# Rows of negated maxima of a second attention: identity products at partitions 32 to 96 exchanged for transposes at partition 0

## The reference, cut to what matters

```python
q = (src @ Wq).reshape(Bb, Tt, H, DH).transpose(0, 2, 1, 3)
k = (src @ Wk_c @ Wk).reshape(Bb, Tt, H, DH).transpose(0, 2, 1, 3)
v = (src @ Wv_c @ Wv).reshape(Bb, Tt, H, DH).transpose(0, 2, 1, 3)
q = _apply_rope(q, sin, cos)
k = _apply_rope(k, sin, cos)
attn = jnp.einsum('bhqd,bhkd->bhqk', q, k) / np.sqrt(DH).astype(np.float32)
attn = jax.nn.softmax(attn, axis=-1)
sa = jnp.einsum('bhqk,bhkd->bhqd', attn, v)
```

## Time and profile before

| | before |
|---|---|
| median of 3 runs | 423.7 us (422.77 to 424.12) |
| the profiled execution, its own time | 420.97 us |
| its span, first to last instruction | 419.2 us |
| mean granted TensorE clock | 0.917 |
| busy: PE / PEld / DVE / ACT / POOL | 363.3 / 195.0 / 297.1 / 234.7 / 162.3 us |
| second attention in the span | about 205 to 353 us |

### The profile page before, as it was taken

The page is one execution under the profiler, slowest core; times in us unless marked ns, Lnnn a source line. Parts: engine busy times, 40 slices in busy tenths (PEclk is TensorE's granted clock), DMA queues, the critical chain, the costliest instruction groups (busy, mean ns, idle before and its releaser), DMA issues.

```text
span 419.2 us, 12911 instructions
## 1 busy us (share of the span) xinstructions
PE 363.3 (87%) x5331; PEld 195.0 (47%) x5331; DVE 297.1 (71%) x538; ACT 234.7 (56%) x489; POOL 162.3 (39%) x342
## 2 busy tenths in 40 slices
PE   8666779999999999997989889779989998999993
PEld 4232345767676767654655333312333333463441
DVE  5995865766878788888698987656787752426565
ACT  2623675767676667666744676545767884422200
POOL 7272163737677576554570111200001160143423
PEclk9985556999999999999999999955999999989997
DMA  7400000000000001000000000500000000000000
GB/s 236 126 22 4 1 5 4 5 23 6 4 9 3 8 6 30 4 4 2 3 5 2 4 25 0 163 1 2 2 0 3 3 0 2 0 2 0 0 25 27
DMA packets 11992, 8.09 MB, mean 19 GB/s; under 512 B 4446, under 2 KB 11022, under 8 KB 11806
## 3 DMA queue, kind: packets, MB, share of 16 engines
q1 hardware_dynamic: 11934, 7.27, 6.0%
HBM read 5.94 MB, written 0.52 MB: 15 GB/s over the span
## 4 chain that ended last, share of the span: by engine, by line
PE 56%; DVE 21%; issue 7%; ACT 7%; POOL 3%; SPq 2%; DMA 2%; ACTq 0%; POOLq 0%; DVEq 0%
PE ps L1236 8%; PE ps L1331 7%; PE ps L1149 5%; PE ps L1198 5%; PE ps L1180 4%; PE ps L1161 4%; DVE m_qk L863 3%; PE ps L1207 3%; PE ps L1223 3%; PE ps L1119 3%; ACT arena L696 3%; PE ps L1021 3%; PE ps L1216 2%; DVE m_qk L860 2%; DVE k_op L820 2%
## 5 line engine op out<-in xcount | busy, mean ns | idle before, releaser
L860 DVE TENSOR_REDUCE m_qk<-ps 128x2 f32<-128x1024 f32 x64 | 76.9, 1220 | 18.9 <-PE ps L1119 18.7
L863 DVE TENSOR_REDUCE m_qk<-ps 128x2 f32<-128x1024 f32 x64 | 76.8, 1219 | 17.6 <-PE ps L1207 17.3
L696 ACT ACTIVATE arena<-ps 128x512 f32<-128x512 f32 x128 | 69.5, 595 | 23.3 <-PE ps L1161 22.7
L711 ACT ACTIVATE arena<-ps 128x512 f32<-128x512 f32 x128 | 67.7, 600 | 17.6 <-PE ps L1223 16.9
L606 POOL TENSOR_TENSOR arena<-arena,eb 128x256 f32<-128x256 f32 x64 | 46.9, 733 | 59.5 <-ACT eb L684 33.2
L684 ACT ACTIVATE eb<-ps 128x512 f32<-128x512 f32 (+1 forms) x64 | 31.3, 542 | 28.7 <-PE ps L1149 28.7
L449 POOL TENSOR_SCALAR var<-mv 128x1 f32<-128x1 f32 (+1 forms) x14 | 2.7, 194 | 107.0 <-ACT eb L753 71.7
L1236 PE MATMUL ps<-arena,v_sb 128*20 128x256 f32 x512 | 41.1, 407 | 2.4 <-DVE arena L868 2.4
L1180 PE MATMUL ps<-arena,v_sb 128*20 128x128 f32 x1024 | 40.8, 284 | 0.0
L607 POOL TENSOR_TENSOR arena<-arena,eb 128x192 f32<-128x192 f32 x64 | 38.6, 603 | 0.0
L1149 PE MATMUL ps<-q_op,rel_k 49*128 49x24 bf16 (+1 forms) x1024 | 31.0, 222 | 6.4 <-ACT arena L696 3.2
(11 more groups left out here) (217 smaller groups left out, 537.9 us busy)
## 6 DMA issues: line engine op xcount, KB each, us to landing
rel_v<-in_relv_ext SPq DMA_DIRECT2D x1, 1024.0 KB, 7.9
eb<-in_w SPq DMA_DIRECT2D x2, 512.0 KB, 5.9
x_sb<-in_x SPq DMA_DIRECT2D x2, 256.0 KB, 3.1
q_op<-farT SPq DMA_DIRECT2D x32, 3.0 KB
q_op<-farT SPq DMA_DIRECT2D x32, 1.5 KB
out<-x_sb SPq DMA_DIRECT2D x8, 64.0 KB, 1.6
rows<-in_rows SPq DMA_DIRECT2D x1, 448.0 KB, 5.7
sel<-in_sel SPq DMA_DIRECT2D x1, 384.0 KB, 3.8
```

What stands on the lines that cost most here:

```text
L696: act.activation(p_ring[:, k % SLOTS_P, e, :], ps[:, bank, :], ACT.Exp).then_inc(sm["bank_free"], 1)
L711: act.activation(p_ring[:, v % RING, e, :], ps[:, bank, :], ACT.Exp).then_inc(sm["bank_free"], 1)
L860: dve.tensor_reduce(m_qk[:, u, n:H:PAIRS], ps[:, banks, :], AX_X, ALU.max).then_inc(sm["pair_free"], 1)
L863: dve.tensor_reduce(m_qk[:, IT * b + n, 2 * p:2 * p + 2], ps[:, banks, :], AX_X, ALU.max).then_inc(sm["pair_free"], 1)
```

## The change

The step `neg` uses the transpose form of the matmul in place of the product with the identity, and always writes partitions 0 and 1 of the bank. ACT reads them there and writes one of three blocks of 512 columns at partitions 0 and 1 in SBUF, where before it wrote partitions 32, 64 or 96 of one block. To have room for the three blocks, `m_rel`, `ends` and `far_bf` of the first attention become views of one tile `far_sb`, and the blocks lie over them; `neg_mT` keeps a tile of its own. The list of steps, the banks, the semaphores and what waits for them stay as they are: each engine issues as many instructions as before, in the same order (PE 4 for each of the 16 steps `neg`).

```diff
-        m_rel = sb("m_rel", [P, NT, H])
         m_rel_bf = sb("m_rel_bf", [P, NT, H], BF16)
-        ends = sb("ends", [P, NT, 2, H])
-        far_bf = sb("far_bf", [P, NT, 2, 2, 3, PAIRS], BF16)
+        far_sb = sb("far_sb", [P, 768])
...
-        neg_rows = sb("neg_rows", [P, 2, 2, P], BF16)
+        neg_mT = sb("neg_mT", [H, 2, 2, P], BF16)
...
-        neg_mT, nm_T = neg_rows[0:H], neg_rows[:, :, :, :].rearrange("p k n t -> p (k n t)")
+        ends = far_sb[:, 0:256].rearrange("p (u c h) -> p u c h", u=NT, c=2)
+        m_rel = far_sb[:, 256:384].rearrange("p (u h) -> p u h", u=NT)
+        far_bf = far_sb[:, 384:768].bitcast(BF16).rearrange("p (u c e s a) -> p u c e s a", u=NT, c=2, e=2, s=3)
+        nm_T = far_sb[0:2, :].bitcast(BF16).rearrange("d (r t) -> d r t", r=3)
...
                 if kind == "neg":
                     b, p = divmod(u, PAIRS)
-                    j = 32 * (1 + u % 3)
                     sp.wait_ge(sm["bank_free"], ring[(kind, u, n)] + 1)
-                    sp.dma_start(q_op[KR + 1:P:64, p, b * S:b * S + S], nm_T[j:j + 2, :]).then_inc(sm[rope_rows[u % 3]], 16)
+                    sp.dma_start(q_op[KR + 1:P:64, p, b * S:b * S + S], nm_T[:, u % 3, :]).then_inc(sm[rope_rows[u % 3]], 16)
...
                 if kind == "neg":
-                    bank, j = emptied(kind, u, n), 32 * (1 + u % 3)
+                    bank = emptied(kind, u, n)
                     if u >= 3:
                         act.wait_ge(sm[rope_rows[u % 3]], 16 * (u // 3))
-                    act.activation(nm_T[j:j + 2, :], ps[j:j + 2, bank, :], ACT.Identity, scale=-1.0).then_inc(sm["bank_free"], 1)
+                    act.activation(nm_T[:, u % 3, :], ps[0:2, bank, :], ACT.Identity, scale=-1.0).then_inc(sm["bank_free"], 1)
...
                 if kind == "neg":
                     b, p = divmod(u, PAIRS)
-                    j = 32 * (1 + u % 3)
                     pe.wait_ge(sm["pair_free"], pair[("max2", u, IT - 1)] + 1)
                     bank = bank_of(kind, u, n)
                     for it in range(IT):
-                        i = pe.matmul(ps[j:j + 2, bank, it * P:it * P + P], m_qk[:, IT * b + it, 2 * p:2 * p + 2], ident[:, :], start=True, stop=True)
+                        i = pe.transpose(ps[0:2, bank, it * P:it * P + P], m_qk[:, IT * b + it, 2 * p:2 * p + 2], ident[:, :])
                     i.then_inc(sm["bank_full"], 1)
```

## The result

| | before | changed |
|---|---|---|
| median | 422.2 us (20 runs, 419.1 to 427.4) | 417.9 us (20 runs, 413.2 to 424.3) |
| ratio to before | | 0.9878, 95% interval 0.9848 to 0.9908 |
| span of the profiled execution | 419.2 us | 422.4 us |
| its mean granted clock | 0.917 | 0.885 |

The forecast was 5.1 us. The profiled execution of the changed kernel is longer than that of before all the same: it had more time at TensorE's lower clock level than most (its 21 executions with a recorded clock have a median of 0.912).

The account below looks back on a forecast made before the run. PE was taken to bound the second attention at 13 of 16 steps, alone from 292 us and with DVE close before 265. Late 3.5 plus early 1.6 us made 5.1, so 423.7 becomes 418.6 us, range 414.8 to 422.3.

Parts of the forecast that it names:

- Half the records: Step `neg` on PE: 4 records where 8 stood, so 64 for the line in place of 128.
- the transposes run as before: Rival: the short outputs take two passes each, records stay at 128, nothing changes, 423.7 us; chance 0.08.
- The price of a step: PE time of a step `neg`: 0.97 us falls to 0.20 + 3 x 0.075 = 0.43 us, saving 0.54 us.
- The upper end of the bound, 0.59 us: Longest time expected for a step `neg`, from line 1247's four transposes of 128 columns; it would save 0.38 us.
- The mixed steps: Three steps, near 219, 292 and 298 us, whose records mix with products with V: each saves 0.41 us (0.25 to 0.54).
- Where it lands: Second attention: steps before 265 us count half, 1.6 us, as DVE is next; those from 292 us count fully, 3.5 us.
- ACT: ACT's idle time before its negation falls from 19.2 us to about 11; not counted again in the sum.
- The stretches that were to show it: Sign: first to last `neg` after 292 us shorter by about 3.5 us, the stretch before 265 us by 1 to 2.
- DVE takes over: Rival: gaps closed on PE reopen before DVE's maxima; only three last steps land, 1.6 us, 422.1 us; chance 0.14.
- Place, copy, shared tile at nothing: Copy source on partitions 0 and 1 and writes to `far_sb` cost nothing; if cover failed, at most 1.6 us.
- The clock takes it back: Rival: too little PE work after 292 us brings a second half-clock stretch, costing 8.7 us, 427.3 us; chance 0.05.
- The tiling rule: Danger: if two-row outputs at partition 0 also lost transpose mode for f32, the sum would be nothing instead of 5.1 us.

Follow-up runs that it names:

- the repeat: The changed kernel run again with no further edit: 417.9 us, ratio 0.9868 to before; its trace has a span of 416.3 us at clock 0.908.
- products_at_0: The changed kernel with identity products at partition 0 in place of the transposes: 421.1 us, ratio 0.9957 to before.
- transposes_twice: The changed kernel with each transpose issued twice, so a step has 8 records again: 422.6 us, ratio 0.9993 to before.
- one_transpose: The changed kernel with one transpose of 8 columns per step in place of four of 2, and ACT negating 8 x 128: 417.7 and 418.1 us in two runs.
- one_transpose_filled: one_transpose with one unused bf16 matmul of 512 columns in front of each transpose: 417.3 us, ratio 0.9908 to before.
- the other two: The changed kernel and one_transpose, each with unused bf16 matmuls of 512 columns in batch 0's values, queries and keys: 422.5 and 424.8 us, ratios 0.9993 and 0.9903.

## Why the prediction was right, and where it was not

- **The total, 5.1 us, and the median, 418.6 us.** Measured 5.2 us by the ratio and 417.9 us. Right, but with luck in it: two terms were off in opposite directions.
- **Half the records.** Right: 64. The rival that the transposes run as before is out.
- **The price of a step.** This term was too good: 0.43 us was forecast, 0.53 measured, so a step saves 0.44 us and not 0.54. What failed is the subtraction: I took line 1247's spacing of 0.13 us and took off 55 ns for a narrower weight load. The spacing is 0.11 us with 2 columns of weights and only 0.13 with 128, so the narrower load saves 0.02 us and not 0.055. The spacing goes with the columns that stream through: in the timeline of before four passes of line 1296, with 512 columns of f32 where these have 128, take 1.92 us, 0.48 each. The 0.11 us was to be had from line 1216 itself, whose passes are as far apart.

```profile
260.39 1.98 PE L1296 MATMUL ps<-xnT,spare 128*128 128x512 f32 x4
262.31 1.03 PE L1216 MATMUL ps<-ident,m_qk 128*2 128x128 f32 x8
```

  The upper end of the bound, 0.59 us, held the value. The mixed steps saved 0.31 us and not 0.41, for the same reason.
- **Where it lands.** The total share was about right, but the split was wrong. I gave the early steps half (1.6 us) since DVE would be next, and the late ones full price (3.5 us). The early steps gave 2.7 to 3.3 us, and the late ones 1.8 to 2.3. With the measured prices its own rule gives (5 x 0.44 + 0.31) / 2 = 1.3 us early and 5 x 0.44 + 2 x 0.31 = 2.8 us late, 4.1 in all. So the halving of the early steps is the other term that failed: it was too low by 1.5 us or more and made up for the price. At the measured saving the eight early steps make 7 x 0.44 + 0.31 = 3.4 us, nearly all of which lands; of the late 6 x 0.44 + 2 x 0.31 = 3.3 us about two thirds do. One of the late steps, at 305 us, was rightly not counted: PE waits for DVE right behind it, 0.59 us before and 1.03 in the repeat, so its 0.44 us became a wait:

```profile
306.63 0.63 PE L1247 MATMUL ps<-ident,arena 128*128 128x128 f32 x4 [0.59 <-DVE arena L868]
```
```profile
306.07 0.63 PE L1246 MATMUL ps<-ident,arena 128*128 128x128 f32 x4 [1.03 <-DVE arena L868]
```

  The 4.3 us that led to the halving are the wait of line 863 alone. DVE was idle for 55 - 46.6 = 8.4 us of that stretch, so there was more room than the forecast allowed; which of it was used no run shows. The profile bears out that DVE comes next, but only for a part: the weight loads of line 1207 waited 8.5 us for the maxima of line 863 before and 11.2 after, while DVE's wait for PE went from 17.3 to 15.7 us. The lines of line 863's view for before and the repeat:

```profile
  PE ps L1207: 17.3, 27
...
  PEld ps L1207: 8.5, 17
```
```profile
  PE ps L1207: 15.7, 28
...
  PEld ps L1207: 11.2, 20
```

- **ACT.** Its wait for the step went down by 4.6 us, not by 8: a step is done 0.44 us earlier, and in two of the 14 places it no longer waits at all. As said, it is the same time seen from ACT.
- **The stretches that were to show it.** From the first `neg` after 292 us to the last it was 49.7 us before and 49.1 in the repeat, and from 212 to 262 us 50.2 in both, but the repeat had 0.97 and 0.90 of the clock there where before had 1.00. Taken out as above, they are 1.5 and 3.1 us shorter, and not 3.5 and 1 to 2: the same split.
- **DVE takes over.** It did not. The forecast of that rival also miscounts: from 322 to 342 us there are four steps `neg`, not three, so it would have been 2.2 us, 421.5.
- **Place, copy, shared tile at nothing.** Right within 0.3 us, by products_at_0.
- **The clock takes it back.** For the changed kernel it did not: 77 against 75 us at the lower level. The reason given for that rival, that transposes weigh less for the clock, found no support: transposes_twice, with 128 transposes for 128 passes of products, spent 76 us there, as before within the uncertainty of 3 us. The Trainium skill, "TensorE: Matmul & The Clock Gate", Part 4, says that a transpose does not count as work for the clock in the way a matmul does. Here the transposes of transposes_twice are 16 x 0.97 = 15.5 us among other work, and at that amount no effect shows. But the rival's pattern did show up where the step was made shorter still, in one_transpose, and there it ate about the whole further gain. My price for it was too high: 20 us at the lower level were to cost 8.7 us, 0.43 us each, while the executions show 0.30. That not all that time waits for PE may be the reason: PE was busy in 16.1 of the 20 us.
- **The tiling rule.** The rule of the Trainium skill, "TensorEngine Tiling (Array Packing)", Restrictions, that column tiling turns off transpose mode for f32 input was weighed as a danger for two rows at partition 0. The 64 records of one pass each show that these do run as transposes. Transposes at partitions 32 to 96 were not tried, so no run here shows the rule itself.

Left open: why one_transpose has 11 us more at the lower clock than before. That it idles more on PE is a guess: one_transpose_filled does not decide it, and the fillers of the other two stood elsewhere.

## What to carry to other kernels

A product with the identity in f32 runs in two passes and a transpose in one of the same length, so with the output at partition 0 the exchange halved the passes here and took a step from 0.97 to 0.53 us; count the passes from the records of the line itself and take their spacing from its own starts. Before crediting a saving on TensorE, write down each execution's span and mean clock: one slope for all executions told 1 us apart here, where medians of 12 differ by chance by as much and a single pair of traces pointed the wrong way. And a stretch in which a second engine is 85% busy can still return most of what is taken off the first; only an experiment on that stretch alone gives its share. Last, look in the trace for the instructions that an experiment adds: a filler in the wrong batch gave a time that looked like an answer.

## What the runs showed of the hardware that was not expected

- f32 transposes of 2 columns begin 0.11 us apart, as passes of a product of 2 columns do. The 0.53 us of four is 0.43 us of these and 0.10 us up to the next matmul of another form.
- Products with an output of 2 rows mix in PE with the products with V behind them, whose outputs start at partitions 0, 32, 64 and 96 in turn: 1.84 us for work that takes 1.97 apart, with the 2 rows at partition 0 as at 64. Transposes do not (1.53 us, which is 0.53 + 1.00).
- The time at the lower clock varies between executions of one kernel by some 30 us (63 to 96 us for before), and each microsecond of it goes with 0.30 us of the kernel's time.
